# Matmuls of a fused transformer kernel on TensorE split at 256 columns, and met waits added until a slot holds 768 instructions

## What is computed

```python
def attn_layer(x, Wqkv, qs, ksc, Wo):            # x: (4, 512, 128)
    q, k, v = split(x @ Wqkv, 3)                 # each 16 heads x 64 = 1024 columns
    q = rotate(l2norm(q) * qs); k = rotate(l2norm(k) * ksc)
    out = local_attention(q, k, v)               # windows of 32 queries, 64 keys
    return out.reshape(b, n, 1024) @ Wo

def ffn_layer(x, g, bln, W1, b1, W2, b2):
    xn = layernorm(x) * g + bln
    a, gate = split(xn @ W1 + b1, 2)             # 341 columns each
    return a * gelu(gate) @ W2 + b2

for i in range(6):
    x = attn_layer(shift_tokens(x), ...) + x
    x = ffn_layer(shift_tokens(x), ...) + x
```

## Time and profile before

| | us |
|---|---|
| median of 3 runs | 2114.34 |
| lowest, highest | 2112.93, 2118.89 |
| the profiled execution | 2119.18 |
| its span (first to last instruction) | 2117.4 |
| granted TensorE clock, mean over the span | 0.984 |

### The profile page before, as it was taken

How to read it: one execution, slowest core, us unless ns; L and a number is a source line. 1 busy time by engine, 2 the same in 40 slices (tenths; PEclk the granted TensorE clock), 3 DMA queues, 4 the chain that set the end, 5 groups by cost and what they waited for, 6 DMA issues and landing times.

```text
span 2117.4 us, 89360 instructions
## 1 busy us (share of the span) xinstructions
PE 1943.4 (92%) x37572; PEld 1442.3 (68%) x37572; DVE 1821.4 (86%) x3995; ACT 1546.8 (73%) x3028; POOL 1290.5 (61%) x1551
## 2 busy tenths in 40 slices
PE   6888899987788999999999999999999999999996
PEld 4666664455566777777777777777777777777774
DVE  6788775577798999999899999999999998998994
ACT  4777763355576877888788887888878878777873
POOL 1111110000378888788787888878888887777771
PEclk9999999998899999999999999999999999999998
DMA  5000000100232322332333323333233332222321
GB/s 117 2 2 2 2 32 31 61 1 1 58 86 70 79 68 70 93 84 67 78 83 78 87 65 77 86 89 79 67 81 83 87 75 63 73 75 73 77 63 41
DMA packets 99377, 132.62 MB, mean 63 GB/s; under 512 B 29052, under 2 KB 44034, under 8 KB 98978
## 3 DMA queue, kind: packets, MB, share of 16 engines
q1 hardware_dynamic: 98978, 126.90, 23.6%
HBM read 28.20 MB, written 1.11 MB: 14 GB/s over the span
## 4 chain that ended last, share of the span: by engine, by line
PE 48%; DVE 23%; ACT 10%; issue 9%; SPq 5%; POOL 3%; DMA 2%; DVEq 0%; POOLq 0%; ACTq 0%
PE pj L630 15%; PE oo L630 15%; ACT arena L1961 7%; PE sc L630 6%; PE tr L1057 5%; DVE arena L1764 4%; DVE arena L1766 4%; SPq L555 3%; PE tr L633 3%; DMA slab<-arena 2%; DVE bv L1772 2%; DVE arena L1521 2%; DVE small L1795 1%; DVE xn L1353 1%; ACT L1965 1%
## 5 line engine op out<-in xcount | busy, mean ns | idle before, releaser
L1961 ACT ACTIVATE arena<-tr 128x512 f32<-128x512 f32 (+3 forms) x894 | 458.8, 562 | 100.0 <-PE tr L633 51.3
L2397 POOL TENSOR_TENSOR arena<-arena 128x1024 f32<-128x1024 f32 x192 | 457.4, 2382 | 91.3 <-DVE arena L1766 87.5
L1961 ACT ACTIVATE arena<-pj 128x512 f32<-128x512 f32 x576 | 332.5, 599 | 150.9 <-PE pj L630 96.1
L2415 POOL TENSOR_TENSOR arena<-arena,small 128x1024 f32<-128x1024 f32 x192 | 365.6, 1904 | 28.1 <-POOL small L2408 0.9
L1961 ACT ACTIVATE arena<-arena 128x1024 f32<-128x1024 f32 (+4 forms) x446 | 304.6, 693 | 87.6 <-DVE arena L1521 74.0
L1772 DVE TENSOR_REDUCE bv<-arena 128x8 f32<-128x512 f32 x384 | 252.7, 679 | 2.9
L630 PE MATMUL oo<-slab,arena 64*32 64x64 f32 (+1 forms) x12416 | 232.7, 229 | 10.5 <-issue 9.7
L2364 POOL TENSOR_SCALAR rstd<-mv 128x4 f32<-128x4 f32 x40 | 11.4, 284 | 364.5 <-DVE mv L1347 364.4
L633 PE MATMUL tr<-ident,arena 128*128 128x128 f32 x1346 | 206.4, 280 | 19.4 <-DMA beta<-in_L_attn_betas 9.9
L630 PEld LDWEIGHTS oo<-slab,arena 64*32 64x32 f32 (+1 forms) x12416 | 160.8, 106 | 80.0 <-issue 44.4
L633 PEld LDWEIGHTS tr<-ident,arena 128*128 128x128 f32 x1346 | 163.3, 143 | 58.3 <-issue 23.9
(11 more groups left out here) (340 smaller groups left out, 4465.0 us busy)
## 6 DMA issues: line engine op xcount, KB each, us to landing
slab<-arena SPq DMA_DIRECT2D x576, 128.0 KB
slab<-arena SPq DMA_DIRECT2D x336, 64.0 KB
arena<-gate_mem SPq DMA_DIRECT2D x24, 256.0 KB, 4.4
wqkv<-in_L_ffn_Wqkv SPq DMA_DIRECT2D x36, 128.0 KB, 2.5
arena<-in_L_ffn_Wqkv SPq DMA_DIRECT2D x36, 128.0 KB, 2.3
wo<-in_L_ffn_Wo SPq DMA_DIRECT2D x24, 128.0 KB, 2.5
w<-in_L_ffn_W SPq DMA_DIRECT2D x6, 341.0 KB, 3.6
YT<-in_L_attn_x SPq DMA_DIRECT2D x4, 256.0 KB, 3.9
```

The costliest lines, as they stand in the source:

```text
L1961: return nc.scalar.activation(o, i, f, **k)
L2397: p_.tensor_tensor(r_, r_, rb[:, k, :], ALU.add).then_inc(sum_ok, 1)
L2415: p_.tensor_tensor(r3, r3, rs[:, k, :].unsqueeze(2).broadcast_to([P, HL, DL]), ALU.mult).then_inc(qk_rdy, 1)
```

## The change

Three things, all on TensorE's list. In `project` the passes c = 0, 1, 2 and 5 are done in two halves of 256 columns: three matmuls for the first half of the bank, then three for the second. In `ff_up` each group of three goes in two halves of 256 tokens, and the wait for `hb_l` now stands ahead of the third matmul of the first half. And `spread_out` puts pairs of waits that are met long before into three places of a slot, SPARE of them in all (17, 19, 19, 10 for t = 0 to 3, and other numbers in the first eight slots).

```diff
--- before.py
+++ after.py
@@ -97,6 +97,9 @@
         self.eng.wait_ge(self.sem, self.base + self.n)
 
 
+
+SPARE_AT = (17, 19, 19, 10)
+SPARE = {0: 0, 1: 0, 2: 11, 3: 42, 4: 42, 5: 43, 6: 43, 7: 24}
 
 PTR = 6
 NMAX = 2 * H0 * T
@@ -1040,11 +1043,13 @@
                     wait(pe, v_cp, g * 2 - 1 + c)
                 else:
                     pe.wait_ge(rot_ev, g * 4 + c - 1)
-                x_, w_ = slice(t * P, (t + 1) * P), slice(c % 2 * S, (c % 2 + 1) * S)
-                k = c // 2
-                mm(pj[:, c % 2], xs_hi[:, x_], high_[k][:, w_], stop=False)
-                mm(pj[:, c % 2], xs_hi[:, x_], low_[:, k, w_], start=False, stop=False)
-                mm(pj[:, c % 2], xs_lo[:, x_], high_[k][:, w_], start=False).then_inc(pj_mm, 1)
+                x_, k, n = slice(t * P, (t + 1) * P), c // 2, S // (2 if c in (0, 1, 2, 5) else 1)
+                parts = [(slice(o, o + n), slice(c % 2 * S + o, c % 2 * S + o + n)) for o in range(0, S, n)]
+                for o_, w_ in parts:
+                    mm(pj[:, c % 2, o_], xs_hi[:, x_], high_[k][:, w_], stop=False)
+                    mm(pj[:, c % 2, o_], xs_hi[:, x_], low_[:, k, w_], start=False, stop=False)
+                    last = mm(pj[:, c % 2, o_], xs_lo[:, x_], high_[k][:, w_], start=False)
+                last.then_inc(pj_mm, 1)
 
             def turn_rows(rows, done, ready, first, second):
 
@@ -1117,17 +1122,26 @@
             def ff_up(m, k, bank):
                 w = CH[k][1]
                 for half, o in ((1, DI + CH[k][0]), (0, CH[k][0])):
-                    mm(bank[0:w, half], w1_hi[:, o:o + w], hB_hi[:, :], stop=False)
-                    mm(bank[0:w, half], w1_lo[:, o:o + w], hB_hi[:, :], start=False, stop=False)
-                    if half:
-                        pe.wait_ge(hb_l, m + 1)
-                    last = mm(bank[0:w, half], w1_hi[:, o:o + w], hB_lo[:, :], start=False)
+                    tok = [slice(u * S // 2, (u + 1) * S // 2) for u in range(2)]
+                    for u in tok:
+                        mm(bank[0:w, half, u], w1_hi[:, o:o + w], hB_hi[:, u], stop=False)
+                        mm(bank[0:w, half, u], w1_lo[:, o:o + w], hB_hi[:, u], start=False, stop=False)
+                        if half:
+                            pe.wait_ge(hb_l, m + 1)
+                        last = mm(bank[0:w, half, u], w1_hi[:, o:o + w], hB_lo[:, u], start=False)
                 last.then_inc(w1_mm, 1)
+
+            def spread_out(n):
+
+                for _ in range(n):
+                    pe.wait_ge(ld_const, n_const)
+                    pe.wait_ge(ld_late, n_late)
 
             def slot(s_):
                 l, b, t, n, g = s_.l, s_.b, s_.t, s_.n, s_.g
                 new, c_, d_, m1, m2 = s_.new, s_.c_, s_.d_, s_.m1, s_.m2
                 n2, t2 = (n, t - 2) if t >= 2 else (n - 1, t + 2)
+                spare = SPARE.get(g, SPARE_AT[t])
                 weighted_ = min(g - 2, NTILE)
 
                 def queries(c):
@@ -1197,6 +1211,7 @@
                 if b == 0 and t == 0:
                     pe.wait_ge(wl_ok[0], l + 1)
                 queries(0)
+                spread_out(spare // 3)
                 if s_.mw is not None:
                     if b == 0 and t == 3:
                         pe.wait_ge(ld_wo, (l + 1) * G * 16)
@@ -1206,11 +1221,13 @@
                         pe.wait_ge(gelu_ev, gated(m2, 2))
                     wait(pe, on_ok, g * 2 - 4)
                     wo_quarter(s_.mw, s_.iw)
+                spread_out(spare // 3)
                 if t == 3 and m1 is not None:
                     pe.wait_ge(t_sub, g - 1)
                     pe.wait_ge(xs_part, m1 * T + T)
                     norm_in(LNB, LNB_BANKS[0], xsF)
                 queries(1)
+                spread_out(spare - spare // 3 * 2)
                 if g > 0:
                     crossing(g, 1)
                 if g == 1:
```

## The result

The change made the kernel slower. The changed kernel takes 2140.31 us (median of 4 runs, 2134.76 to 2147.54), the kernel before took 2116.61 us in the runs beside it (2112.93 to 2122.27). The ratio is 1.0112, with a 95% interval of 1.007 to 1.0153. The forecast was 2093. The medians differ by 24 us, the two profiled executions, from which all rows come, by 18.

A forecast was written before the change was run, and what follows sets the result against it. TensorE, 96% busy from 640 to 2060 us, was taken to set the pace. 2119.2 - 27 + 5 + 1 = 2098 against the profiled execution, 2093 us against the runs' median of 2114.3; 8-in-10 range 2084 to 2108.

The forecast's parts named there:

- B: Page boundary in `values_(1)`, some 60 to 77 instructions into its 128; forecast not to stall.
- wrong: Signs against the forecast, among them an issue stall at one place of every slot, in `values_(1)` above all.
- A: Page boundary in the turned probabilities or at `project(2)`, 11 to 27 instructions ahead of the `pt_cp` wait; forecast not to stall.
- Alignment: 768 instructions a slot fix the page boundaries; all 30.3 us of TensorE's issue stalls go, worth -27 us.
- the first rival: Other waits take over: TensorE meets busy DVE or ACT more often, half of the 27 is lost, 2107; chance 0.13.
- Halves: 1,584 more matmuls on TensorE, at 0.003 us a split: +5 us.
- The rival of 0.018: Fixed cost of a matmul: 0.018 us for each split, +29 us for the halves, time 2117; chance 0.09.
- Added waits: 17 to 19 a slot (t < 3), never waited for, costing only the time of passing them: +1 us.
- The boundary at A is too close to the wait: Next page is fetched only after the `pt_cp` wait; 2111 if 11 instructions are too few, 2147 if 14 are; chance 0.05.
- The rule of the Trainium skill: Rival: instruction refill is hidden, the stalls have another cause that the alignment doesn't touch, 2120; chance 0.04.
- decided between 2 and 11: How many instructions from boundary to `pt_cp` wait suffice: at 2 the next boundary stalled 0.89 us, at 11 to 30 none.

The follow-up runs named there:

- e2: The changed kernel with the third group of added waits taken from ahead of `probs` and the first two groups made longer; ratio to the kernel before 1.0024.
- e5: As e2, but no added waits in the first slots except 4 in slot 0, and three slots without halves; A at instruction 84; ratio to before 0.9996.
- e7: As e5, with one more slot without halves and 16 waits in slot 0, so boundaries stand 12 instructions later, A at 96; ratio to before 1.0092.
- e11: As e9, with one added wait of a slot moved directly ahead of `project(2)`, making the `rot_ev` wait an instruction of its own; ratio to before 1.0101.
- e14: As e11, with the two waits ahead of `project(2)` swapped: the long-met one is an instruction, the weight load carries `rot_ev`; ratio to before 1.01.
- e13: e9 with the order of waits of e12; ratio to the kernel before 0.9979, 2108.96 us beside 2114.22.
- e9: As e5, with 44 more added waits in the last four slots, moving the boundaries at the program's end 44 instructions earlier; ratio to before 0.9963.
- e12: The changed kernel with the waits ahead of `values_(0)` in another order, `pt_cp` first and carried by a weight load; ratio to before 1.0023.
- e15: As e12, with fewer waits in the first slots, so all boundaries stand 15 instructions later, A at 106; ratio to before 1.0018.
- e4: The changed kernel with 24 more waits in two early slots, so all boundaries from the seventh slot on stand 24 instructions earlier; ratio to before 1.017.
- e8: As e5, with the boundaries 36 instructions earlier, A at 48; ratio to the kernel before 1.0039.

## Why the prediction was wrong

**Boundaries and pages.** Right: 256 instructions, 318 packets, and nearly all stalls of the steady slots at B (45.3 of 46.4 us), the place named under "wrong".

**The step that failed** is the one at A: "behind A the list halts at `pt_cp` for as long as the turned probabilities take, and so the next page is fetched meanwhile". The fetch doesn't begin in that halt; it begins 1.0 us or more behind it, in 61 of 64 slots of the changed kernel. In the slots of before on which I built, the page came at 3.3 to 4.15 us for another reason than that halt: their A stands ahead of the `rot_ev` load, little behind the one that carries `e_exp` or ahead of it, and no wait instruction lies between. I had read them as "11 to 30 instructions ahead of the `pt_cp` wait", and A of the changed kernel has 11 to 14 too. The same rows could be read by what stands between, and there the bad one is behind the `rot_ev` load and the good ones ahead of it. The halt doesn't keep a page away as such: in e2 and e5 the transfer begins within it in 42 and 58 of 64 slots, in the changed kernel in 1, in e7, e11 and e14 in none, and it is the same wait instruction in all of them. Why the list's passing A ahead of it isn't enough in the latter stays open.

**What undid it in the change** is twofold. With t = 0, A stands behind the `rot_ev` load. With t = 1, 2 it stands one or two instructions ahead, but the third group of waits fills the time from 2.3 us on with wait instructions, makes `e_exp` one of them, and lets the list reach A only at 3.2 us. Taking the group away mended t = 1, 2 and not t = 0 (e2); A ahead of the `rot_ev` load mended both (e5), 12 instructions on neither (e7).

**The sum by its terms.**
- *Alignment*, forecast -27: over the 84 slots the stalls for issue grew by 18.3 us (26.4 to 44.7), the waits for DVE and ACT fell by 8.7 (19.0 to 10.3), the gaps under 0.15 us by 3.8, and TensorE's busy time grew by 4.1, which makes the 9.8. Where A is placed right the term is real but smaller: the 84 slots gain 12.1 (e5) to 16.7 us (e13) net of the halves, since the waits for ACT grow from 8.4 to 12.6 us (e5). That is the first rival, which I gave half of 27, and it took less.
- *Halves*, forecast +5: they start 0.12 apart, not 0.117. Six matmuls of 512 columns in a row (`project(5)` and `queries(0)`) take 1.498 us to the next operation, the twelve halves 1.528: 0.005 a split, 8 us in all; by busy time it is 4 us in the 84 slots. The rival of 0.018 is out.
- *Added waits*, forecast +1: ahead of `tr` nothing sticks out, as forecast. What the third group does to the fetch with t = 1, 2 (e2) wasn't in the term at all; I had priced the time of passing them, not what the list is late for behind them.
- *First slots and the end* had no term: +3.5 and +4.8. The count 768 fixes the phase of the drain too, and put two boundaries where they stall (moving them, e9, took the end from 107.1 to 102.2).

**The rivals.** "The boundary at A is too close to the wait" came true in its place and nearly in its time: 2147 if t < 3 all stall, against 2140. The nearness is in part luck, since it sums 0.75 a stall where 0.6 was measured with a gain of 21 where the steady slots had none. I gave it 0.05 because one slot at 2 instructions stalled and seven at 11 or more didn't. The distance to the `pt_cp` wait didn't decide it: at 13 or 14 instructions the same slots are late in the changed kernel and early in e2. The rule of the Trainium skill ("Runtime: NRT & Kernel Launch", Instruction fetch mechanics), that crossing a block costs a tail-bump of a queue and is mostly hidden, doesn't fit this trace: 46 us of 1360 are lost at the boundaries here. By the rule e5 and e7 would take the same time; they differ by 1%.

## What to carry to other kernels

Where an engine's list is thousands of short instructions, ask of each page boundary what the list does around it: where it lay close to a weight load that held for some 0.7 us, with no wait instruction behind it for a dozen instructions, the page came in time; where wait instructions followed, or the boundary lay farther on, it came behind the next long halt. Look then at the dense work one page on, and place boundaries by that; the program's end needs its own look. Before reading a rule off slots that went well, list everything that those slots share, above all which waits were still holding, by the times at which their semaphores fill: two that fill 0.01 us apart (`rot_ev` and `e_exp` here) are easily taken for each other. And after changing the order of waits, look which of them holds now. And a rival that is "decided between 2 and 11" by eight samples deserves more than 0.05 when the forecast hangs on it.

## What the hardware showed unexpectedly

- In the late slots of the changed kernel (t < 3) a page's transfer begins 1.0 to 2.0 us behind the end of the `pt_cp` wait at 4.60 us. Behind the end of the last wait instruction it is 1.07 us in the middle, and 1.04 to 1.11 in e2, e7, e11, e12, e14 and e15.
- One wait instruction more, met or not, between the boundary and the `rot_ev` load made the page late in 85 of 85 slots (e11, e14); without it the page came early in 59 of 64 slots of t < 3 (e5).
- Met wait instructions follow each other in TensorE's list 0.105 us apart, while the list passes pairs of matmuls into the queue far faster: the 28 instructions between two groups in e4 took 0.11 us.
- Open is what the request itself waits for. A boundary passed early, with wait instructions behind it and a halt at `v_cp` (e8), has its page early too, and how far behind a held weight load the list is read meanwhile no row shows. A run with A 15 to 17 instructions behind the `e_exp` load and still ahead of the `rot_ev` load would tell the two readings apart.
